# Feed-forward gate product in three passes of rounded halves, and a later split of the second context block in the first attention batch

## What is computed

```python
x = x + cross_attention(layernorm(x), ctx)   # 16 batches, 2048 keys each, 16 heads of 32
x = x + mamba_and_mlp(layernorm(x))          # state space, then w2 . gelu(w1 . z), RMS norm
x = x + ffn(layernorm(x))
# ffn, with xf = layernorm(x):
scores = softmax(xf @ W_gate)                # W_gate is 512 x 7 here
w = top_2(scores); w = w / w.sum()           # their sum weighs the expert's product
out = xf @ W_shared.T + w.sum() * (xf @ W_expert.T) + bias
```

## Time and profile before

| | |
|---|---|
| median of 3 runs | 3971.57 us (3971.56 to 3974.35) |
| the profiled execution, its own time | 3968.16 us |
| its span, first to last instruction | 3966.1 us |
| PE busy | 3831.3 us, 97% of the span |
| DVE, ACT, POOL busy | 2832.1, 1752.0, 1285.5 us |
| mean granted clock of PE | 0.990 of full |

### The profile page before, as it was taken

One profiled execution on the slowest core, in us unless ns is written; L12 is line 12 of the kernel. 1 busy time (PEld: TensorE's weight loads), 2 busy tenths in 40 slices (PEclk: granted clock), 3 DMA queues, 4 the chain that ended last, 5 costly groups with the idle time before them and its releaser, 6 DMA issues.

```text
span 3966.1 us, 83590 instructions
## 1 busy us (share of the span) xinstructions
PE 3831.3 (97%) x34880; PEld 2811.2 (71%) x34880; DVE 2832.1 (71%) x2964; ACT 1752.0 (44%) x3490; POOL 1285.5 (32%) x604
## 2 busy tenths in 40 slices
PE   8999999999999999999999998999999998799998
PEld 6777777878878777777877775555555554388886
DVE  5577667667667767767766766999999999844443
ACT  2334324424424423433432445777777778422221
POOL 1111111011011111111111103888888889821011
PEclk9999999999999999999999998999999999999999
DMA  4110111011011111011011122202221022120000
GB/s 157 38 44 29 39 54 32 26 54 32 26 54 32 36 44 44 26 41 44 29 39 51 34 70 89 56 14 62 59 59 55 21 64 86 46 70 21 33 27 17
DMA packets 96901, 183.73 MB, mean 46 GB/s; under 512 B 8449, under 2 KB 12929, under 8 KB 96546
## 3 DMA queue, kind: packets, MB, share of 16 engines
q1 hardware_dynamic: 96546, 178.27, 13.9%
HBM read 152.82 MB, written 25.43 MB: 45 GB/s over the span
## 4 chain that ended last, share of the span: by engine, by line
PE 85%; POOL 6%; DVE 5%; ACT 2%; issue 2%; DMA 1%; DVEq 0%; POOLq 0%; ACTq 0%; SPq 0%
PE scores L527 36%; PE scores L602 8%; PE o_acc L616 7%; PE b_y L1447 6%; PE c_acc L1964 4%; PE c_ring L1949 4%; POOL b_drive L1012 3%; PE scores L596 3%; PE scores L571 3%; DVE b_decay L1302 3%; PE b_work L1359 3%; PE b_work L1408 2%; PE c_experts_ps L1996 1%; PE b_work L1344 1%; POOL b_drive L984 1%
## 5 line engine op out<-in xcount | busy, mean ns | idle before, releaser
L244 POOL TENSOR_TENSOR c_lo<-c_raw,c_hi 128x2048 fp32r<-128x2048 f32 x64 | 294.6, 4604 | 1930.8 <-DVE c_hi L346 1930.8
L407 DVE TENSOR_REDUCE max_parts<-scores 128x2 f32<-128x1024 f32 x512 | 603.6, 1221 | 213.3 <-PE scores L571 213.3
L434 DVE TENSOR_TENSOR prob_sums<-prob_sums,probs 128x1024 f32<-128x1024 f32 x480 | 566.8, 1222 | 115.0 <-ACT probs L319 115.0
L1012 POOL TENSOR_TENSOR b_drive<-b_dt_u,b_bc 128x1024 f32<-128x1024 f32 x256 | 600.0, 2359 | 111.6 <-PE b_y L1447 77.7
L319 ACT ACTIVATE probs<-scores 128x512 f32<-128x512 f32 x1024 | 529.0, 604 | 215.1 <-PE scores L602 215.1
L1447 PE MATMUL b_y<-b_drive,b_ident 128*128 128x512 f32 x1024 | 498.7, 617 | 70.0 <-DVE b_drive L1313 48.7
L1302 DVE TENSOR_TENSOR_SCAN b_decay<-b_decay,b_drive 128x1024 f32<-128x1024 f32 x217 | 496.5, 2288 | 12.4 <-ACT b_decay L1170 8.7
L304 ACT ACTIVATE k_hi<-scores,bk_sb 128x512 fp32r<-128x512 f32 x256 | 176.4, 689 | 608.2 <-PE scores L527 608.2
L1170 ACT ACTIVATE b_decay<-b_dt,b_a 128x254 f32<-128x254 f32 x1024 | 425.2, 461 | 0.4
L312 ACT COPY v_sb<-scores 128x512 f32<-128x512 f32 x240 | 140.9, 587 | 635.8 <-PE scores L527 635.8
L1447 PEld LDWEIGHTS b_y<-b_drive,b_ident 128*128 128x128 f32 x1024 | 188.8, 194 | 297.8 <-issue 161.3
(11 more groups left out here) (231 smaller groups left out, 6521.8 us busy)
## 6 DMA issues: line engine op xcount, KB each, us to landing
c_raw<-in_ctx SPq DMA_DIRECT2D x64, 1024.0 KB, 5.2
b_bc<-bc_scratch SPq DMA_DIRECT2D x128, 256.0 KB, 4.3
c_w_raw<-in_mlp_w SPq DMA_DIRECT2D x16, 512.0 KB, 3.6
q_scratch<-v_sb SPq DMA_DIRECT2D x4, 1024.0 KB, 4.3
q_raw<-q_scratch SPq DMA_DIRECT2D x16, 256.0 KB, 5.2
q_raw<-in_x SPq DMA_DIRECT2D x16, 256.0 KB, 2.9
x_scratch<-q_raw SPq DMA_DIRECT2D x16, 256.0 KB, 5.8
attn_scratch<-attn_out_sb SPq DMA_DIRECT2D x16, 256.0 KB, 2.0
```

Source lines behind the costliest of these rows:

```text
L244: pool.tensor_tensor(c_lo[:, slot], c_raw[:], c_hi[:, slot].bitcast(F32), ALU.subtract).then_inc(c_lo_ready, 1)
L407: dve.tensor_reduce(max_parts[:, g, 2 * pair:2 * pair + 2, s], max_banks[:, 2 * pair:2 * pair + 2, :], AX.X, ALU.max).then_inc(max_taken, 1)
L434: dve.tensor_tensor(part, part, probs[:, u % 4], ALU.add).then_inc(summed, 1)
L1012: pool.tensor_tensor(drive[:, m % 4], dt_u[:, 2 * p:2 * p + 2, :].unsqueeze(1).to_broadcast([P, SG, 2, T]), bc[:, g, 0].unsqueeze(2).to_br ...
```

## The change

In attention, batch 0 only, DVE's `high_part` of block 1 moves from behind `low_keys` 0 to behind `reduce_max` 2. Two semaphores of the query weights become one.

In the feed-forward stage W_gate is split once, in the first step, by `split_gate` on DVE between `high_shared` and `split_zm(1)`: a memset, a rounding copy and a subtraction. `gate` becomes 16 matmuls of one pass: for each of two groups, 4 of 16 columns (`xf_hi` by both halves of W_gate side by side) and 4 of 8 columns (`xf_lo` by the high half). It waits for `xf_lo` and not for `xf_t`. `take_gate` adds the two parts. The pieces move: PE_GATE 8 to 9, ACT_EXP 10 to 11, DVE_GATE 9 to 10, DVE_WEIGHTS 11 to 12, the first of DVE_OUT 11 to 12. PE_SHARED and PE_EXPERT stay. The load of W_shared counts on the same semaphore as those of W_gate and W_expert, so `high_shared` waits for all three.

```diff
@@ run_vector of attention, batch(), s loop @@
                     low_keys(n, s, 0)
-                    if s == 0:
-                        if not first:
-                            dve.wait_ge(proj_ready, n * 2 * chunks)
+                    if s == 0 and not first:
+                        dve.wait_ge(proj_ready, n * 2 * chunks)
                         high_part(n + 1, (s + 1) % 2)
                     low_keys(n, s, 1)
...
                         reduce_max(i, s, g)
                         if g + 2 < chunks:
                             low_keys(n, s, g + 2)
+                        if first and s == 0 and g == 2:
+                            high_part(n + 1, (s + 1) % 2)
@@ feed_forward @@
-    PE_TURN, PE_GATE, PE_SHARED, PE_EXPERT = 6, 8, (9, 12), (11, 13)
-    ACT_SQUARES, ACT_XF, ACT_EXP, ACT_SCALE = 1, 7, 10, 2
+    PE_TURN, PE_GATE, PE_SHARED, PE_EXPERT = 6, 9, (9, 12), (11, 13)
+    ACT_SQUARES, ACT_XF, ACT_EXP, ACT_SCALE = 1, 7, 11, 2
-    DVE_ADD, DVE_X2, DVE_XF, DVE_GATE, DVE_WEIGHTS, DVE_OUT = 0, 3, 5, 9, 11, (11, 14)
+    DVE_ADD, DVE_X2, DVE_XF, DVE_GATE, DVE_WEIGHTS, DVE_OUT = 0, 3, 5, 10, 12, (12, 14)
...
-            sp.dma_start(w_s_raw[:], w_shared_t.rearrange("(k p) o -> p k o", p=P)).then_inc(w_s_loaded, 16)
+            sp.dma_start(w_s_raw[:], w_shared_t.rearrange("(k p) o -> p k o", p=P)).then_inc(experts_loaded, 16)
...
-        CONSTS_LOADED, EXPERTS_LOADED = 3 * 16, 2 * 16
+        CONSTS_LOADED, EXPERTS_LOADED = 3 * 16, 3 * 16
...
             def high_shared():
-                dve.wait_ge(w_s_loaded, 16)
+                dve.wait_ge(experts_loaded, EXPERTS_LOADED)
                 for n in range(2):
                     dve.tensor_copy(w_s_hi[:, 2 * n:2 * n + 2, :], w_s_raw[:, 2 * n:2 * n + 2, :]).then_inc(w_s_high, 1)
+
+            def split_gate():
+                dve.wait_ge(experts_loaded, EXPERTS_LOADED)
+                dve.memset(w_g_parts[:].bitcast(F32), 0.0).then_inc(w_g_split, 1)
+                dve.wait_ge(w_g_split, 1)
+                dve.tensor_copy(w_g_parts[:, :, 0, 0:gates], w_g[:]).then_inc(w_g_split, 1)
+                dve.wait_ge(w_g_split, 2)
+                dve.tensor_tensor(w_g_parts[:, :, 1, 0:gates], w_g[:], w_g_parts[:, :, 0, 0:gates].bitcast(F32),
+                                  ALU.subtract).then_inc(w_g_split, 1)
...
-                dve.tensor_copy(logits[:, :, 0:gates],
-                                turned_ps[:, 0, 0:group * 8].rearrange("p (b e) -> p b e", e=8)[:, :, 0:gates]
-                                ).then_inc(gate_taken, 1)
+                parts = turned_ps[:, 0, 0:group * 16].rearrange("p (b n e) -> p b n e", n=2, e=8)
+                chain(dve.tensor_copy(logits[:, :, 0:gates], parts[:, :, 0, 0:gates]))
+                dve.tensor_tensor(logits[:, :, 0:gates], logits[:, :, 0:gates], parts[:, :, 1, 0:gates], ALU.add
+                                  ).then_inc(gate_taken, 1)
...
                         if m == hidden_chunks - 1:
                             high_shared()
+                            split_gate()
...
             def gate(t):
-                pe.wait_ge(experts_loaded, EXPERTS_LOADED)
-                pe.wait_ge(xf_t_ready, (t + 1) * group)
-                for b in range(group):
+                pe.wait_ge(w_g_split, GATES_READY)
+                pe.wait_ge(xf_lo_ready, t + 1)
+                for b in range(group):
+                    cols, at = slice(b * P, (b + 1) * P), b * 16
                     for k in range(chunks):
-                        ins = pe.matmul(turned_ps[:, 0, b * 8:b * 8 + gates], xf_t[:, k, b * P:(b + 1) * P],
-                                        w_g[:, k, :], start=(k == 0), stop=(k == chunks - 1))
+                        pe.matmul(turned_ps[:, 0, at:at + 16], xf_hi[:, k, cols],
+                                  w_g_parts[:, k].rearrange("p n e -> p (n e)"), start=(k == 0), stop=False)
+                    for k in range(chunks):
+                        ins = pe.matmul(turned_ps[:, 0, at:at + 8], xf_lo[:, k, cols], w_g_parts[:, k, 0, :],
+                                        start=False, stop=(k == chunks - 1))
                 ins.then_inc(gate_ready, 1)
```

More of the change, by code:

```diff
@@ L133, in cross_attention @@
         wq_loaded, x_loaded = sem("q_weights_loaded"), [sem(f"q_x_loaded_{i}") for i in range(q_steps)]
-        wq_high, wq_low = sem("q_weights_high"), sem("q_weights_low")
+        wq_split = sem("q_weights_split")
         stats_ready, moments_ready, rstd_ready = sem("q_stats_ready"), sem("q_moments_ready"), sem("q_rstd_ready")
@@ L374, in run_vector @@
             dve.wait_ge(wq_loaded, 16)
-            dve.tensor_copy(wq_hi, wq).then_inc(wq_high, 1)
+            dve.tensor_copy(wq_hi, wq).then_inc(wq_split, 1)
             low_queries(0)
-            dve.wait_ge(wq_high, 1)
-            dve.tensor_tensor(wq_lo, wq, wq_hi.bitcast(F32), ALU.subtract).then_inc(wq_low, 1)
+            dve.wait_ge(wq_split, 1)
+            dve.tensor_tensor(wq_lo, wq, wq_hi.bitcast(F32), ALU.subtract).then_inc(wq_split, 1)
             normalise(1)
@@ L498, in project_queries @@
                         if n == 0:
-                            pe.wait_ge(wq_high, 1)
+                            pe.wait_ge(wq_split, 1)
                             pe.wait_ge(xn_hi_ready, (i + 1) * group)
                         if n == 1:
-                            pe.wait_ge(wq_low, 1)
+                            pe.wait_ge(wq_split, 2)
                         if n == 2:
@@ L1499, in feed_forward @@
     LAG = 3
+    GATES_READY = 3
     piece = 2
@@ L1520, in feed_forward @@
         b2_sb, norm_sb, bias_sb = sb("c_b2", [P, width]), sb("c_norm", [P, width]), sb("c_bias", [P, width])
-        w_g = sb("c_w_g", [P, chunks, gates])
+        w_g, w_g_parts = sb("c_w_g", [P, chunks, gates]), sb("c_w_g_parts", [P, chunks, 2, 8], F32R)
         mean_sq = sb("c_mean_sq", [P, group])
@@ L1578, in feed_forward @@
         xf_turned, xf_t_ready, xf_lo_ready = sem("c_xf_turned"), sem("c_xf_t_ready"), sem("c_xf_lo_ready")
-        w_s_loaded, w_s_high, w_s_split = sem("c_w_s_loaded"), sem("c_w_s_high"), sem("c_w_s_split")
-        gate_ready, gate_taken = sem("c_gate_ready"), sem("c_gate_taken")
+        w_s_high, w_s_split = sem("c_w_s_high"), sem("c_w_s_split")
+        gate_ready, gate_taken, w_g_split = sem("c_gate_ready"), sem("c_gate_taken"), sem("c_w_g_split")
         logits_ready, exp_ready = sem("c_logits_ready"), sem("c_exp_ready")
@@ L1788, in run_vector @@
             dve.wait_ge(ready, 6)
-            TAIL_LINKS = group + 10
+            TAIL_LINKS = group + 11
             def high_w2(n):
```

## The result

The changed kernel takes 4004.76 us (median of 6, 4003.93 to 4007.71) against 3972.14 us before (median of 6): ratio 1.0082, 95% interval 1.0072 to 1.0092. That is slower by 32.6 us where 27 were forecast, and inside the range. The profiled execution took 4004.95 us, 36.8 more than the one of before, which at 3968.16 us lay under all six that make the median of before.

The account below looks back on a forecast made before the run. PE, busy 97% of the span, was taken as the bound, so its waits add in full. -4.2 + 18.8 + 8.0 + 2.7 + 2.3 = +27.6 us, a median near 3998 us; range 3980 to 4010.

Parts of the forecast that it names:

- Visit 12: Feed-forward, seven steps: PE's shared of group 1 waits 2.7 us for DVE's later finish, +18.8 us.
- The clock: Behind the visit 12 waits: PE falls to 1.2 GHz after five of seven, 1.6 us each, +8.0 us.
- Rival A: Feed-forward: stalls as forecast but no lower clock behind them, +19.6 us, 3991; chance 0.18.
- Splitting W_gate: First feed-forward step: DVE's small copy and subtraction are held by POOL's subtractions, PE waits, +2.7 us.
- Rival B: First feed-forward step: POOL doesn't hold small instructions, +24.9 us, 3996; chance 0.70 together with the forecast.
- The tail: End of the feed-forward: gate now waits for xf_lo with nothing to hide it, +2.3 us.
- Attention: Batch 0: block 0's stall goes, a 1.25 us wait behind block 2's later load comes, net -4.2 us.
- The gate's product: Feed-forward gate: still 16 passes bound by weight loads, so zero change; bounds -0.6 and +6.8 us.
- Rivals C and D: C: no PE wait in visit 12, 3972, chance 0.08; D: also gate passes at half cost, 3965, chance 0.04.

Follow-up runs that it names:

- e6: Changed kernel with DVE's weights back in visit 11 and the first finish left in 12: 3988.78 us, 17.4 over the kernel before.
- e3: Changed kernel with split_gate ahead of high_shared: 3995.99 us, 25.8 over the kernel before.
- e5: Kernel before with only DVE's weights and first finish moved from visit 11 to 12: 3998.53 us, ratio 1.0072.
- e4: Changed kernel with ten useless matmuls of 512 columns on PE ahead of shared of group 1 in visit 12: 3990.06 us, 19.8 over the kernel before.
- e2: Changed kernel with DVE's weights and first finish back in visit 11: 3972.09 us, ratio 1.0001 to the kernel before.
- e7: Changed kernel with weights and first finish in visit 11, split_gate ahead of high_shared, group 0's expert product ahead of the tail's gate: 3965.79 us, ratio 0.9987.
- e1: Kernel before with the attention part of the change alone: 3966.15 us, ratio 0.9989.
- e8: e7 with high_part of block 1 in batch 0 behind the second visit's maxima, not the third's: 3964.43 us, ratio 0.9982.

## Why the prediction was right

The sum was +27.6 and the medians say +32.6. The mechanism came as it was forecast, the wait of `shared` for `finish` in visit 12 above all; two terms were too small, the clock's and W_gate's. Term by term, against the trace of the changed kernel:

- **Visit 12**, forecast 2.7 us a step, 18.8. The chain is the one that was worked out, instruction by instruction. PE is idle 2.52 and 2.53 us; with the 0.16 us to the end of the matmul ahead of it that is the 2.69 which the sum counted to the start of PE's next matmul. It counted nothing for the slower first four, 0.12 (e6). So it is 2.8 a step, 20 us, as the steps without a fall of the clock in e3 and e5 and the filled ones of e4 show (2.8 to 2.9 each). e2 and e5 settle that it comes from two numbers.
- **The clock**, forecast 5 of 7 at 1.6, 8.0. This is the term that was mis-sized most: seven of seven fell, the third for twice as long. Of the 31.9 us that the steps add, 31.9 - 7 x 2.8 = 12 are the clock, which e4 gives back. The price of a fall, 1.6, was about right; the number of falls was not. It was taken from stalls of 2.67 us in the state space, and waits of 2.52 us between the denser matmuls of the feed-forward were followed by a fall 19 times of 21 (seven of seven, and six of seven in e3 and in e5). Whether the two stages differ or five of seven was a low draw isn't shown. Waits of 1.40 to 1.76 us were followed by none in seven (e6). Rival A is out.
- The Trainium skill (TensorE: Matmul & The Clock Gate, "Why this matters for your kernels") asks for no idle gaps above about 3 us between bursts of matmuls, by which this term would have been zero. The traces do not agree: here 2.52 us were enough 19 times of 21, and the measurement decides.
- **Splitting W_gate**, forecast 2.7, with a fall of the clock only in its upper bound of 4.3. PE waited 2.23 us and the clock fell: `c_xf` goes from -1.5 to +2.6, 4.1 us. e3 shows that the hold is POOL's, for an instruction of 28 columns as for one of 1024. Rival B is out.
- **The tail**, forecast 2.3; measured 36.8 - 34.5 = 2.3. PE's wait is 3.85 us where it was 1.44, and e7 hides it.
- **Attention**, forecast -4.2; alone (e1) it is -4.1 in the medians and -4.7 to -4.8 in the trace. The new wait behind the late load was forecast at 1.25 us and is 0.8 to 0.9. In the changed kernel's profile only 1.5 of it is left at the start of the feed-forward: that is the drift between executions of the last section, which no term of the sum allowed for.
- **The gate's product**, forecast zero. Its 16 passes take 1.70 us (3530.42 to 3532.12) where they took 1.71, and the first four matmuls behind them, of 512 columns here, take 1.16 us against the usual 1.08, the same 0.08 more as before: zero it is. (Its upper bound was written 0.05 x 16 x 8 = 6.8; that product is 6.4, and 6.8 comes of 0.16 - 0.107.)
- Rivals C and D needed PE not to wait in visit 12, and fall with it.

With the measured terms the sum is -4.1 + 20 + 12 + 4.1 + 2.3 = 34.3 against 32.6 in the medians; the 1.7 between them lies within the interval of their ratio, some 4 us either way.

## What to carry to other kernels

When work is laid by hand into numbered visits of several engines, a number moved on one engine must be checked against who waits for it in the same visit on the others: here DVE's `finish` went behind work that depends on PE's visit 12, and PE asks for it in visit 12. Where TensorE is the bound, a wait cost its idle time and 0.3 us more, and behind waits of 2.5 us nearly always (of 1.4 us in none of seven) a stretch at the low clock as well, which was more than half as dear again (12 us on 20). A tiny VectorE instruction in SBUF can cost microseconds (2.40 us for 0.18) if it starts right behind the signal that lets GpSimd go; put it in front of that signal.

## What the runs showed of the hardware that was not expected

Ten useless matmuls of 512 columns in a wait of 2.5 us made the kernel faster by some 13 us, because the clock stayed up.

The time moves by some microseconds from one profiled execution to the next in stages where the kernels don't differ. The start of the feed-forward lies at -4.6 in e1 and at +2.9 in e6, though batch 0 of attention differs by only 1.0 between them. Most of it comes in the state space: from batch 15 to the feed-forward the shift changes by -0.7 us in e1 and by +4.7 in e6 and e7. The clock falls at other places there. Over 3098:3114 the granted clock reads 0.79 in e2, e6 and e7, where the shift grows by 3.5, 4.7 and 4.7, and 1.00 in all others. Over 2970:2990 it reads 1.00 in these three and in the changed kernel (+1.6), and 0.91 in the others, where the shift changes by -0.7 to +0.2, but in e8 by +2.8. So the drift goes with where the falls land, though e8 doesn't fit, and that they are its cause was not tested. Part of the drift, up to 2 us, comes earlier, in steps of 0.2 to 0.9 us in single batches of attention in which the clock is at full; what these are was not tried and stays open.
